# A linear-attention and mixture-of-experts kernel: two buffers for the expert rows, an earlier x2hat, and V's products in halves

## The reference

```python
# x, ctx: (32 sequences, 128 tokens, 128); 16 heads of width 8
x = x + xattn(layernorm(x), ctx, ctx)
x = x + ffn(layernorm(x))

def xattn(q_in, k_in, v_in):              # causal linear attention
    q, k, v = q_in @ Wq + bq, k_in @ Wk + bk, v_in @ Wv + bv
    qp, kp = elu(q) + 1, elu(k) + 1
    # sums_t = sum over s <= t of kp_s v_s^T ; res_t = sums_t . qp_t
    return (res / cumsum(qp, axis=1)) @ Wo + bo

def ffn(h):                               # 8 experts, the top 2 of each token
    bids = sigmoid(h @ conf_w.T + conf_b) * wealth
    top, sel = top_k(bids, 2)
    w = softmax(top)                      # combine weights
    return sum over the two chosen experts e of w_e * (silu(h @ gate_e.T) * (h @ up_e.T)) @ down_e.T
```

## Time and profile before

| | before |
|---|---|
| time, median of 3 runs | 441.85 us |
| the profiled execution's own time | 443.99 us |
| its span, first to last instruction | 442.2 us |
| busy: PE, DVE, ACT, POOL | 334.8, 299.5, 217.5, 211.1 us |
| granted TensorE clock, mean | 0.84 of full |
| body 5 (oT at 145.64 us to oT at 169.74 us) | 24.10 us |

### The profile page before, as it was taken

One profiled execution on the slowest core, in us unless ns is written; L12 is line 12 of the kernel. 1 busy time (PEld: TensorE's weight loads), 2 busy tenths in 40 slices (PEclk: granted clock), 3 DMA queues, 4 the chain that ended last, 5 costly groups with the idle time before them and its releaser, 6 DMA issues.

```text
span 442.2 us, 12750 instructions
## 1 busy us (share of the span) xinstructions
PE 334.8 (76%) x4555; PEld 277.3 (63%) x4555; DVE 299.5 (68%) x809; ACT 217.5 (49%) x440; POOL 211.1 (48%) x343
## 2 busy tenths in 40 slices
PE   2677878786987878697630199999999999989700
PEld 2356565655856566576320079999999999967500
DVE  4357899969698897969509157676676676644336
ACT  2462656538364755633122046667667666644300
POOL 5010214737264573737666306666666565665400
PEclk9997989788766979858555579999999999999955
DMA  8102121320404031101012412122222222111069
GB/s 273 48 1 80 44 77 45 95 75 32 140 14 155 3 90 45 38 14 33 25 42 66 115 26 65 56 72 62 63 69 66 65 67 58 55 50 28 6 218 351
DMA packets 25676, 32.40 MB, mean 73 GB/s; under 512 B 3718, under 2 KB 19340, under 8 KB 25616
## 3 DMA queue, kind: packets, MB, share of 16 engines
q1 hardware_dynamic: 21296, 23.11, 17.0%
q0 software_dynamic: 4320, 8.47, 5.8%
HBM read 19.81 MB, written 12.21 MB: 72 GB/s over the span
## 4 chain that ended last, share of the span: by engine, by line
issue 29%; POOL 25%; DVE 16%; PE 14%; DMA 8%; ACT 4%; SPq 2%; POOLq 1%; DVEq 0%; ACTq 0%
POOL by_token L490 12%; POOL by_expert L422 8%; DMA by_expert<-token_rows,rows_to 4%; DVE Pm L714 3%; PE scores L967 3%; PE bank L951 3%; DVE Vexp L697 2%; PE bank L983 2%; DVE stats L649 2%; POOL y_scale L485 2%; DMA w_hi<-by_token 1%; DMA vo_s<-in_vo_pack_dram 1%; PE bank L942 1%; PE bank L1009 1%; POOL rstd L393 1%
## 5 line engine op out<-in xcount | busy, mean ns | idle before, releaser
L490 POOL DMA_INDIRECT by_token<-y_sb,y_to x71 | 82.9, 1168 | 26.9 <-issue 25.2
L903 DVE TENSOR_TENSOR Kexp<-hid,hid_hi 128x512 f16<-128x512 f32 x71 | 48.8, 688 | 39.4 <-ACT hid_hi L628 39.3
L422 POOL DMA_INDIRECT by_expert<-token_rows,rows_to x64 | 64.4, 1006 | 20.2 <-issue 20.2
L621 ACT ACTIVATE silu<-bank 128x512 f32<-128x512 f32 x71 | 42.2, 596 | 35.3 <-PE bank L1098 34.8
L967 PEld LDWEIGHTS scores<-qT,Kexp 32*128 32x128 f32 x1024 | 40.8, 235 | 24.1 <-DVE Pm L714 21.3
L897 DVE SCALAR_TENSOR_TENSOR hid<-scores,silu 128x512 f32<-128x512 f32 x71 | 48.5, 684 | 7.4 <-PE scores L1098 7.4
L967 PE MATMUL scores<-qT,Kexp 32*128 32x128 f32 (+1 forms) x1024 | 45.8, 329 | 9.8 <-DVE Pm L714 9.8
L1113 PE MATMUL bank<-w_hi,hid_hi 128*128 x284 | 51.4, 220 | 2.4 <-DVE Kexp L903 2.4
L1115 PE MATMUL bank<-w_hi,Kexp 128*128 x284 | 51.0, 219 | 0.0
L1114 PE MATMUL bank<-w_lo,hid_hi 128*128 x284 | 50.9, 219 | 0.0
L612 ACT ACTIVATE y_sb<-bank,y_scale 128x128 f32<-128x128 f32 x71 | 22.7, 365 | 48.3 <-PE bank L1115 48.3
(11 more groups left out here) (152 smaller groups left out, 736.9 us busy)
## 6 DMA issues: line engine op xcount, KB each, us to landing
w_raw<-in_w_pack_dram SPq DMA_DIRECT2D x8, 768.0 KB, 5.0
xg<-by_expert SPq DMA_DIRECT2D x31, 130.0 KB
x_all<-in_x_tok_dram SPq DMA_DIRECT2D x8, 256.0 KB, 5.3
cT<-in_ctx_t_dram SPq DMA_DIRECT2D x8, 256.0 KB, 5.5
w_hi<-by_token SPq DMA_DIRECT2D x4, 512.0 KB, 6.7
w_lo<-by_token SPq DMA_DIRECT2D x4, 512.0 KB, 7.2
out_dram<-x_all SPq DMA_DIRECT2D x8, 256.0 KB, 6.0
by_expert<-pad_row SPq DMA_DIRECT2D x9, 130.0 KB, 2.7
```

Source lines behind the costliest of these rows:

```text
L422: pool.indirect_dma_start(by_expert, bass.IndirectOffsetOnAxis(ap=rows_to[:, s, b:b + 1], axis=0), token_rows[:, b, s, :], None).then_inc( ...
L490: pool.indirect_dma_start(by_token, bass.IndirectOffsetOnAxis(ap=y_to[:, kk, s:s + 1], axis=0), y_sb[:, kk, s, :], None, bounds_check=NT * ...
L903: dve.tensor_tensor(hid_lo[:, k % 2, slot, :], hid[:, slot, :], hid_hi[:, k % 2, slot, :], ALU.subtract).then_inc(lo_done, 1)
```

## The change

Four edits, all in the attention stage:

1. `token_rows`, `rows_to` and the semaphore `dispatched` exist twice, by the parity of the unit. The rows of unit u-1 now wait for the dispatch of unit u-3.
2. On ACT, x2hat of the tail (`tail_norm`) stands right behind `off_scores(u, 1)`, ahead of the copy of xT; it was behind `off_scores(u, 2)`.
3. On ACT, the copy of x2T, the exponential of q and the router's exponential follow `off_scores(u, 2)` in this order; the exponential of q was ahead of `off_scores(u, 2)`.
4. V's products are two halves with a semaphore step each. In a body the first half stands between the transposes of x2hat and the logits, the second where the whole stood. `front_v` on DVE waits for each half by itself. At the start of the program the halves wait for k and q of the unit before separately too.

```diff
-        rows_to = sb("rows_to", [P, TOP, UB], U32)
+        rows_to = [sb(f"rows_to{i}", [P, TOP, UB], U32) for i in range(2)]
-        token_rows = sb("token_rows", [P, UB, TOP, ROW])
+        token_rows = [sb(f"token_rows{i}", [P, UB, TOP, ROW]) for i in range(2)]
-        dispatched = sem("dispatched")
+        dispatched = [sem(f"dispatched{i}") for i in range(2)]
...
 # SP, load_unit
-                    sp.wait_ge(v_ps, u - 1)
+                    sp.wait_ge(v_ps, 2 * (u - 1))
...
 # POOL, dispatch
-                        pool.indirect_dma_start(by_expert, bass.IndirectOffsetOnAxis(ap=rows_to[:, s, b:b + 1], axis=0),
-                                                token_rows[:, b, s, :], None).then_inc(dispatched, 16)
+                        pool.indirect_dma_start(by_expert, bass.IndirectOffsetOnAxis(ap=rows_to[u % 2][:, s, b:b + 1], axis=0),
+                                                token_rows[u % 2][:, b, s, :], None).then_inc(dispatched[u % 2], 16)
 # ACT
             def tail_norm(u, par):
                 act.wait_ge(shift2_done, u + 1)
+                if u >= 2:
+                    act.wait_ge(row_lo_done, TOP * (u - 1))
                 norm(x2hat[par], u, rstd2, shift2, x2hat_done)
...
             def tail_rows(u, par):
-                if not first(u):
-                    act.wait_ge(dispatched, 16 * UB * TOP * u)
+                if u >= 2:
+                    act.wait_ge(dispatched[par], 16 * UB * TOP * (u // 2))
...
                 off_scores(u, 1)
+                if not first(u):
+                    tail_norm(u - 1, 1 - par)
                 if not last(u):
                     front_copy_x(u + 1)
                     front_keys(u + 1, 1 - par, range(2))
+                off_scores(u, 2)
+                if not first(u):
+                    tail_x2(u - 1, 1 - par)
+                if not last(u):
                     front_exp(u + 1, 1)
-                off_scores(u, 2)
-                if not first(u):
-                    tail_norm(u - 1, 1 - par)
+                if not first(u):
+                    tail_exp1(u - 1)
                 if not last(u):
                     front_keys(u + 1, 1 - par, range(2, 4))
-                if not first(u):
-                    tail_x2(u - 1, 1 - par)
-                    tail_exp1(u - 1)
                 off_scores(u, 3)
 # DVE
             def front_v(u, par):
-                dve.wait_ge(v_ps, u + 1)
                 for half in range(2):
+                    dve.wait_ge(v_ps, 2 * u + half + 1)
...
-                if not first(u):
-                    dve.wait_ge(dispatched, 16 * UB * TOP * u)
+                if u >= 2:
+                    dve.wait_ge(dispatched[u % 2], 16 * UB * TOP * (u // 2))
 # PE
-            def front_values(u, par):
+            def front_values(u, par, half):
                 pe.wait_ge(ctx_loaded[par], 16 * (u // 2) + 16)
                 if not first(u):
-                    pe.wait_ge(qk_done, 2 * u)
-                for c in range(NCH):
-                    ps = bank[1 - c // 4][:, (c % 4) * P:(c % 4 + 1) * P]
+                    pe.wait_ge(qk_done, 2 * u - 1 + half)
+                for c in range(half * NCH // 2, (half + 1) * NCH // 2):
+                    ps = bank[1 - half][:, (c % 4) * P:(c % 4 + 1) * P]
...
                 if not first(u):
                     tail_x2(u - 1, 1 - par)
+                if u < UNITS - 2:
+                    front_values(u + 2, par, 0)
+                if not first(u):
                     tail_logits(u - 1)
...
-                if not isinstance(u, int) or u < UNITS - 2:
-                    front_values(u + 2, par)
+                if u < UNITS - 2:
+                    front_values(u + 2, par, 1)
```

More of the change, by code:

```diff
@@ L125, in attention_moe_kernel @@
         unit_start = sb("unit_start", [P, UB, TOP])
-        token_rows = sb("token_rows", [P, UB, TOP, ROW])
-        row_halves = token_rows[:].rearrange("p b s r -> p (b s r)").bitcast(F16).rearrange("p (b s r) -> p b s r", b=UB, s=TOP)
+        token_rows = [sb(f"token_rows{i}", [P, UB, TOP, ROW]) for i in range(2)]
+        row_halves = [rows[:].rearrange("p b s r -> p (b s r)").bitcast(F16).rearrange("p (b s r) -> p b s r", b=UB, s=TOP) for rows in token_rows]
         pad_row = sb("pad_row", [P, ROW])
@@ L358, in load_tile @@
                     sp.wait_ge(xgT_ps, i - 3)
-                sp.wait_ge(dispatched, 16 * NB * TOP)
+                for rows in dispatched:
+                    sp.wait_ge(rows, 16 * NB * TOP // 2)
                 sp.dma_start(xg[:, k, 0:size(i)], by_expert[bass.ds(at, size(i) * P), :].rearrange("(s p) r -> p s r", s=size(i))).then_inc(xg_loaded[k], 16)
@@ L406, in tail_rows @@
                 for s in range(TOP):
-                    pool.tensor_tensor(row_halves[:, :, s, D:2 * D], x2hat[par][:], row_halves[:, :, s, 0:D], ALU.subtract).then_inc(row_lo_done, 1)
+                    pool.tensor_tensor(row_halves[par][:, :, s, D:2 * D], x2hat[par][:], row_halves[par][:, :, s, 0:D], ALU.subtract).then_inc(row_lo_done, 1)
                 if not first(u):
                     pool.wait_ge(id_next, u)
-                pool.tensor_tensor(token_rows[:, :, :, D + 1], pair_id[:], unit_start[:], ALU.add).then_inc(row_id_done, 1)
+                pool.tensor_tensor(token_rows[par][:, :, :, D + 1], pair_id[:], unit_start[:], ALU.add).then_inc(row_id_done, 1)
             def dispatch(u, batches):
@@ L553, in tail_rows @@
                 act.wait_ge(x2hat_done, UB * (u + 1))
-                if not first(u):
-                    act.wait_ge(dispatched, 16 * UB * TOP * u)
-                act.activation(row_halves[:, :, :, 0:D], x2hat[par][:].unsqueeze(2).to_broadcast([P, UB, TOP, D]), ACT.Copy).then_inc(row_hi_done, 1)
+                if u >= 2:
+                    act.wait_ge(dispatched[par], 16 * UB * TOP * (u // 2))
+                act.activation(row_halves[par][:, :, :, 0:D], x2hat[par][:].unsqueeze(2).to_broadcast([P, UB, TOP, D]), ACT.Copy).then_inc(row_hi_done, 1)
             def tail_exp1(u):
@@ L577, in body @@
                     front_keys(u + 1, 1 - par, range(2))
-                    front_exp(u + 1, 1)
                 off_scores(u, 2)
                 if not first(u):
-                    tail_norm(u - 1, 1 - par)
+                    tail_x2(u - 1, 1 - par)
+                if not last(u):
+                    front_exp(u + 1, 1)
+                if not first(u):
+                    tail_exp1(u - 1)
                 if not last(u):
                     front_keys(u + 1, 1 - par, range(2, 4))
-                if not first(u):
-                    tail_x2(u - 1, 1 - par)
-                    tail_exp1(u - 1)
                 off_scores(u, 3)
@@ L767, in tail_weights @@
                 done(dve.reciprocal(wts[:], vdiff[:]))
-                if not first(u):
-                    dve.wait_ge(dispatched, 16 * UB * TOP * u)
-                dve.tensor_scalar(token_rows[:, :, 0, D], wts[:], 1.0 / WSCALE, None, ALU.mult).then_inc(weights_done, 1)
-                dve.scalar_tensor_tensor(token_rows[:, :, 1, D], wts[:], 1.0 / WSCALE, vexp[:], ALU.mult, ALU.mult).then_inc(weights_done, 1)
+                if u >= 2:
+                    dve.wait_ge(dispatched[u % 2], 16 * UB * TOP * (u // 2))
+                dve.tensor_scalar(token_rows[u % 2][:, :, 0, D], wts[:], 1.0 / WSCALE, None, ALU.mult).then_inc(weights_done, 1)
+                dve.scalar_tensor_tensor(token_rows[u % 2][:, :, 1, D], wts[:], 1.0 / WSCALE, vexp[:], ALU.mult, ALU.mult).then_inc(weights_done, 1)
             def tail_place(u):
@@ L783, in tail_place @@
                 with nc.allow_low_precision(reason="a row's number is a whole number, exact in any of the types"):
-                    dve.tensor_reduce(rows_to[:], place[:], AX_X, ALU.add).then_inc(rows_to_done, 1)
+                    dve.tensor_reduce(rows_to[u % 2][:], place[:], AX_X, ALU.add).then_inc(rows_to_done, 1)
             def weights(u, par, m):
@@ L1051, in _ @@
             pe.wait_ge(const_loaded, 16)
-            front_values(0, 0)
+            front_values(0, 0, 0)
+            front_values(0, 0, 1)
             pe.wait_ge(qk_loaded, 16)
@@ L1057, in _ @@
             front_project_q(0)
-            front_values(1, 1)
+            front_values(1, 1, 0)
+            front_values(1, 1, 1)
             scores(0, 0, 0)
```

## The result

The changed kernel takes 457.47 us, median of 4 runs (456.15 to 459.02); the kernel before 441.73 us in the same comparison. The ratio is 1.039, 95% interval 1.029 to 1.048: slower by 3.9%. Executions more than 1.5% above the fastest of their kernel count as a slower state and stay out of all ratios here, and where only two others are left no ratio is given. The forecast was 445.2 us and its range ended at 450.0: the direction was right, the size was not.

The account below looks back on a forecast made before the run. VectorE's work was taken to set the body once the second buffer removes dispatch waits. Start -2.9, body 0 -2.0, bodies 1 to 6 +11.1, body 7 and end -2.9 make +3.3: 445.2 us, range 432 to 450.

Parts of the forecast that it names:

- x2hat ahead of xT: ScalarE waits for shift2, delaying the q product to T = 10.9 from oT; clock falls, VectorE stands 2.2 to 2.3 us.
- The body's 26.5 us: Bodies 1 to 6 take 26.5 us each, bounds 23.9 and 26.8; together +11.1 us.
- the discount of 0.3 us a body: Body taken at 26.5 instead of 26.8 us, since part of the q product may run at full clock.
- 21.96 us as VectorE's own work: Body 5's 24.10 us less its 2.14 us pause ahead of the routing weights, taken as VectorE's work per body.
- rival 2: Slow clock reaches into the next body's head; bodies of 27.9 us, 8.4 us more, 453.6 us in all; chance 0.12.
- today the clock is back before the body ends: Argument against the slow clock reaching round into the head of the next body.
- the standing that I had priced: VectorE stands 2.2 to 2.3 us at mask 2 and 2.5 to 2.6 us at qT in each body.
- Start, -4.9: V in halves gains 2.9 us at the program's start and 2.0 us in body 0.
- Body 7, -0.9: Body 7 has no xT to delay and loses its dispatch wait of 0.94 us.
- The end, -2.0: Behind body 7, sends start some 3 us earlier, so GpSimd is free when unit 7's statistics come: -2.0 us.
- V in halves costs nothing in the bodies: In bodies 1 to 5 V's halves gain nothing and cost nothing as long as the logits are hidden.
- About 0.2%, 0.9 us: Size of difference that this kernel's measurement can tell from no change.

Follow-up runs that it names:

- gap_filled: Changed kernel plus two unused 128x512 products a body on TensorE in the gap ahead of the q product: 439.5 us, ratio 1.006 to the kernel before.
- xT_first: Changed kernel with the copy of xT ahead of x2hat again on ACT, q's exponential still late: 429.3 us, ratio 0.979 to the kernel before.
- act_order: Kernel before with edits 2 and 3 alone, ACT's new order; one buffer, V's products whole: 458.5 us, ratio 1.034 to the kernel before.
- buffers: Kernel before with edit 1 alone, the second buffers; ACT's order and V's products as before: 436.2 us, ratio 0.986 to the kernel before.
- xT_first_filled: Changed kernel, xT copied ahead of x2hat, GpSimd's row work behind the row numbers, three unused products a body ahead of the ranks: 419.8 us, ratio 0.948.
- both_filled: Changed kernel with unused products in two gaps: two a body ahead of the q product, three ahead of the rank products: 433.3 us, ratio 0.988.
- exp_back: Changed kernel with q's exponential ahead of the scores' copy of batch 2 again; x2hat stays ahead of xT: 436.3 us, ratio 0.999.
- halves: Kernel before with edit 4 alone, V's products in halves: 435.3 us, ratio 0.986 to the kernel before.
- act_halves: Changed kernel without the second buffer, so edits 2, 3 and 4: 457.6 us, ratio 1.043 to the kernel before.

## Why the prediction was right in direction and wrong in size

- **x2hat ahead of xT: right.** T = 8.61 for shift2, the gap of 3.3 us, the fall of the clock, and mask 2 at T = 15.5 came as worked out in the three bodies whose head was not late; gap_filled shows that the gap costs time through the clock, xT_first that the order makes the gap. There was luck in the fit: with the same gap in act_order the clock fell some 2.5 us later in the body, and mask 2 came at T = 14.0 to 14.2.
- **The body's 26.5 us: the step that failed.** The bodies took 27.5 to 29.9, together 10.5 us more. Three terms were mis-sized. First, the discount of 0.3 us a body for a q product that is fast in part: it took 2.07 or 2.08 us in all six, which makes 1.8 us. Second, 21.96 us as VectorE's own work: the dispatch wait had kept the weight writes apart from GpSimd's subtraction in five of the six bodies, and without it they take 4.7 us in six bodies and not 6 x 0.17, 3.7 us more (the same appears in buffers alone). Without this overlap the 21.96 is right: in xT_first_filled a body takes 21.9 to 22.2 us. Third, 5.0 us remain for the second fall of the clock, rival 2, which had a chance of 0.12: the three bodies with a slow head are 4.4 us longer together than three of 27.5. gap_filled and both_filled differ by the second filling alone, and it took 3.5 us off their bodies.
- **Rival 2 was priced as an alternative** to the fall in the middle of the body; it came on top of it. The argument against it, "today the clock is back before the body ends", was true of the falls in the middle. In the trace before itself the granted clock was 0.50 from about T = 3 to 9 of bodies 3 and 4, where VectorE waited 0.78 and 0.64 us for a mask. I listed the pause ahead of the ranks in the rival and did not work out its length, 2.6 to 2.75 us in bodies 1 to 6. It is no consequence of the standing that I had priced: xT_first has no standing at mask 2 or qT in bodies 1 to 6, and the pause is 2.8 to 3.1 us. It goes with the late place of q's exponential, since exp_back, which differs from the changed kernel in nothing else, has 1.0 to 1.3 us in bodies 1 to 5.
- **Start, -4.9: measured -7.8.** Unit 0's k product started at 11.03, 0.8 us of it because V's weights arrived earlier in this execution (7.00 against 7.83); the q product ran in 1.12 and not 2.07 us. halves shows the same 37.8, but the fit varies: in the profiles of all kernels with V in halves oT of unit 0 lies between 36.4 and 40.5, and 44.8 or more with V whole.
- **Body 7, -0.9: measured +2.0.** Its head was slow as well (mask 0 waits 1.65 us), and one small operation of VectorE (`vdiff`, 128x4, behind the router's exponential) took 2.01 us beside the subtraction. **The end, -2.0: measured -1.5**, right.
- **V in halves costs nothing in the bodies: wrong under the new order** (167.3 us in act_halves against 162.7 in act_order), right under the old one (147.9 in halves and before).
- **"About 0.2%, 0.9 us" as what the measurement can tell from no change: too small.** It came from three runs that lay close together. The next run of the same kernel took 436.0 us, and over all comparisons its runs took 434.8 to 446.1 us.

What stays open: why equal pauses of TensorE end in a fall of the clock in one body and not in another, or at another moment, no run here shows; the 5.0 us are what is left of a sum and not measured by themselves; and taking the overlap of VectorE and GpSimd away shortened bodies in the profiles, but no comparison of times shows the gain of that by itself.

## What to carry to other kernels

When a step is moved up in an in-order list, look up when its input is ready, and then follow each instruction that now stands behind it to the engine that waits for it. Price a gap on TensorE by what runs behind it at half clock, and then work out the length of every other gap in the body under the new order, before giving a second fall a small chance. To find out what the clock costs, fill a gap with products that nobody needs and compare. A wait that is removed may have kept two engines apart: ask what now runs at the same time.

## What the runs showed of the hardware

In the changed kernel the granted clock fell to 0.50 (1.2 GHz) in or just behind TensorE's gaps of 3.34 us and 1.84 us ahead of the q product and, in bodies 1 to 5, of 2.75 us ahead of the ranks, in body 5 only 1.5 us behind the gap. A gap does not always bring it down: in body 5 of xT_first a pause of 2.97 us ahead of the ranks, and in body 5 of gap_filled one of 2.75 us, passed at 1.00. Twelve unused products in the first gap and 21 in the second brought the ratio from 1.039 to 1.006 and 0.988. The Trainium skill ("TensorE: Matmul & The Clock Gate", section "What's actually happening") puts the ramp penalty, the cost of the slow matmuls before the clock comes up, under 1% of a typical span. This kernel's clock fell twice in most bodies, and filling alone gave 3% and 5%.

VectorE's small operations (128x4 to 128x64) took 0.82, 1.14 and up to 2.01 us when a 128x512 subtraction ran on GpSimd, and 0.16 to 0.23 without it; oT, the statistics and Vexp beside the same subtraction kept their 0.68, 0.28 and 0.42 us. The held operations end within 0.1 us of the end of a subtraction. The Trainium skill ("SBUF — State Buffer", section "SBUF: two separate sides") has the two engines share one pair of ports that an instruction holds until it ends. It names only some forms of VectorE's instructions as users of that pair; the rows agree with it in that some operations were held to the end and others not at all.
